# State-space layers: every state product summed by accumulating transposes, z projected in its own batch

## The reference, cut to what matters

```python
xz = xn @ in_proj; x_in, z = split(xz)            # 512 channels each
u  = silu(causal_conv4(x_in) + conv_b)
dt_r, B, C = split(u @ x_proj)                    # 64, 16, 16
dt = softplus(dt_r @ dt_proj + dt_b); A = -exp(A_log)
h  = h * exp(dt * A) + (dt * u) * B               # scan over tokens, 16 states a channel
y  = sum_n h[n] * C[n] + u * D
out = x + gate * ((y * silu(z)) @ out_proj)
```

## Time and profile before

| | us |
|---|---|
| median of 3 runs | 3429.45 |
| span of the profiled execution | 3412.4 |
| PE / DVE / ACT / POOL busy | 2677.2 / 2564.3 / 2151.3 / 1715.5 |

### The profile page before, as it was taken

The page is one execution under the profiler, slowest core; times in us unless marked ns, Lnnn a source line. Parts: engine busy times, 40 slices in busy tenths (PEclk is TensorE's granted clock), DMA queues, the critical chain, the costliest instruction groups (busy, mean ns, idle before and its releaser), DMA issues. The chain is left out here.

```text
span 3412.4 us, 37646 instructions
## 1 busy us (share of the span) xinstructions
PE 2677.2 (78%) x11156; PEld 1441.3 (42%) x11156; DVE 2564.3 (75%) x3375; ACT 2151.3 (63%) x3536; POOL 1715.5 (50%) x1221
## 2 busy tenths in 40 slices
PE   5787588888888888838888888848877788787875
PEld 4555244444444444422333333224444444444443
DVE  2444288888888898947777777538988888888895
ACT  0333478878878778613555555547876776767772
POOL 0000077867768778930000000027887877877785
PEclk9999699999999999967998989969999899989998
DMA  2000101011111111135444444010111111111111
GB/s 89 25 25 31 66 32 51 32 52 49 42 51 40 44 39 52 39 69 82 76 76 76 75 76 70 20 66 32 48 41 58 53 47 53 40 58 51 41 61 45
DMA packets 104194, 176.59 MB, mean 52 GB/s; under 512 B 10741, under 2 KB 91421, under 8 KB 95166
## 3 DMA queue, kind: packets, MB, share of 16 engines
q1 hardware_dynamic: 99775, 161.69, 17.7%
q0 software_dynamic: 4224, 12.59, 1.2%
HBM read 139.70 MB, written 34.14 MB: 51 GB/s over the span
## 5 line engine op out<-in xcount | busy, mean ns | idle before, releaser
L1037 POOL TENSOR_TENSOR l_h<-l_h,l_c_all 128x512 f32<-128x512 f32 x1024 | 1481.3, 1457 | 459.0 <-DVE l_h L966 430.8
L966 DVE TENSOR_TENSOR_SCAN l_h<-l_dA,l_ps_dbu 128x512 f32<-128x512 f32 x1024 | 1218.3, 1207 | 254.1 <-PE l_ps_dbu L1196 157.2
L838 ACT ACTIVATE l_dub<-l_duT,l_b_tok 128x512 f32<-128x512 f32 x1024 | 726.0, 713 | 336.7 <-PE l_ps_dbu L1196 330.6
L1196 PE MATMUL l_ps_dbu<-ident,l_dub 128*128 128x128 f32 x4096 | 644.7, 291 | 257.6 <-DVE l_h L966 175.6
L1196 PEld LDWEIGHTS l_ps_dbu<-ident,l_dub 128*128 128x128 f32 x4096 | 500.7, 148 | 683.6 <-DVE l_h L966 331.9
L852 ACT ACTIVATE l_dA<-l_dt,l_a_neg 128x512 f32<-128x512 f32 x1024 | 726.4, 713 | 0.2
L1628 ACT ACTIVATE l_probs<-l_ring 128x512 f32<-128x512 f32 x512 | 284.2, 598 | 301.4 <-PE l_ring L1752 298.7
L1183 PE MATMUL l_ps_y<-l_h,ident 128*128 128x512 f32 x768 | 430.2, 644 | 51.9 <-DVE l_h L931 51.4
L1461 DVE TENSOR_REDUCE l_q_max<-l_ring 128x1 f32<-128x512 f32 x512 | 327.5, 681 | 144.1 <-PE l_ring L1745 139.4
L996 POOL DMA_INDIRECT l_x_in<-x_dram,l_idx_x x32 | 37.3, 1166 | 735.9 <-DMA l_idx<-in_idx 729.6
L931 DVE TENSOR_TENSOR l_h<-l_h 128x512 f32<-128x512 f32 x384 | 350.5, 916 | 11.8 <-POOL l_h L1037 11.3
(11 more groups left out here) (237 smaller groups left out, 3000.9 us busy)
## 6 DMA issues: line engine op xcount, KB each, us to landing
...
```

Of the source, the lines that this page charges most:

```text
L838: return act.activation(dub[:, n % 2, t, :], duT[:, p, t, :], ACT.Copy, scale=b_tok[:, p, t, n:n + 1])
L966: dve.tensor_tensor_scan(h[:, h_slot(s), :], dA[:, s % DA_RING, :], ps_dbu[:, dbu_slot(s), :], 0.0, ALU.mult, ALU.add).then_inc(scan_ok, 1)
L1037: pool.tensor_tensor(h[:, h_slot(s), :], h[:, h_slot(s), :], c_all[:, (n // C_GROUP) % 2, n % C_GROUP, :], ALU.mult).then_inc(hc_ok, 1)
L1196: last = pe.transpose(ps_dbu[:, dbu_slot(s), t * P:(t + 1) * P], dub[:, n % 2, t, j * P:(j + 1) * P], ident[:])
```

## The change

`DIRECT`, the pairs and `add_states` go. `sum_states` now handles every unit by `add_turned`: four 128x128 transposes with the product as the stationary operand, which PE accumulates into `ps_y`. `ps_y` is thereby token-major. `SUM_LAG` is 9, and `h` has a ring of 16 slots (`H_RING`) where it had 12. The D term is `u *= D` on POOL in units 52 to 55 (`skip_term`), added by one more `add_turned` per block. `u` has one buffer instead of two. `z` is projected token-major inside its own batch (PE units 0, 2, 4, 6; ACT copies in 1, 3, 5, 7; SiLU in unit 32). `y_gate` comes behind the scans of units 5 to 8, and its token-major result is turned back by PE (`y_turn`, units 14, 18, 22, 26) and copied by ACT (`turned`, units 16, 20, 24, 28). The steps of the next batch keep their unit numbers.

```diff
 UNITS = N * JB
-DA_RING, DBU_RING = 8, 3
-PAIRED = UNITS // 2
-ADD_LAG, SUM_LAG = 3, 7
+DA_RING, DBU_RING, H_RING = 8, 3, 16
+SUM_LAG = 9
...
 def h_slot(s):
 
-    n, j = s // JB, s % JB
-    return 2 * JB + j if n % 2 else n // 2 % 2 * JB + j
...
+    return s % H_RING
...
-        u = sb("u", [P, 2, JB, T])
-        z = sb("z", [P, 2, JB, T])
+        u = sb("u", [P, JB, T])
+        z = sb("z", [P, 2, TB, DI])
...
-        diag_d = sb("diag_d", [P, JB, P])
...
-        h = sb("h", [P, 3 * JB, T])
+        h = sb("h", [P, H_RING, T])
...
-                def z_part(b, p, j):
-                    act.wait_ge(in_mm, b * 2 * JB + 2 * j + 2)
-                    if j == 0:
+                def z_part(b, p, t):
+                    act.wait_ge(z_mm, b * TB + t + 1)
+                    if t == 0:
                         if not early(b):
                             act.wait_ge(y_ok, b * JB - JB)
-                    act.activation(z[:, p, j, :], bank(b, "z", j), ACT.Copy).then_inc(z_ok, 1)
-
-                def silus(b, p):
+                    act.activation(z[:, p, t, :], misc[:], ACT.Copy).then_inc(z_ok, 1)
+
+                def silu_u(b):
                     act.wait_ge(conv_ok, b * JB + JB)
-                    act.activation(u[:, p, :, :], work[:], ACT.Silu).then_inc(u_ok, 1)
-                    act.wait_ge(z_ok, b * JB + JB)
-                    act.activation(z[:, p, :, :], z[:, p, :, :], ACT.Silu).then_inc(u_ok, 1)
-                    act.preload_act_table_set(EXP_LN)
+                    if not first(b):
+                        act.wait_ge(sum_ok, b * UNITS - UNITS + JB + H_RING)
+                    act.activation(u[:], work[:], ACT.Silu).then_inc(u_ok, 1)
+
+                def silu_z(b, p):
+                    act.wait_ge(z_ok, b * TB + TB)
+                    act.activation(z[:, p, :, :], z[:, p, :, :], ACT.Silu).then_inc(zs_ok, 1)
+
+                def turned(b, j):
+                    act.wait_ge(y_tr, b * JB + j + 1)
+                    act.activation(y[:, j, :], misc[:], ACT.Copy).then_inc(yd_ok, 1)
...
-                    if s in (16, 20, 24, 28): z_part(b, p, (s - 16) // 4)
-                    if s == 32: silus(b, p)
...
+                        if s in (1, 3, 5, 7): z_part(b, p, s // 2)
+                        if has_post and s in (16, 20, 24, 28): turned(b - 1, (s - 16) // 4)
+                        if s == 32:
+                            if has_prep:
+                                silu_u(b + 1)
+                            silu_z(b, p)
+                            act.preload_act_table_set(EXP_LN)
...
+                for j in range(JB):
+                    turned(B - 1, j)
...
                 def y_gate(b, p, j):
-                    dve.wait_ge(sum_ok, b * PAIRED + PAIRED - JB + j + 1 + CREDIT)
+                    dve.wait_ge(sum_ok, b * UNITS + UNITS - JB + j + 1 + H_RING)
                     if j == 0:
                         dve.wait_ge(out_mm, b * OUT_PARTS + 1)
-                        dve.wait_ge(u_ok, b * 2 + 2)
-                    dve.tensor_tensor(y[:, j, :], ps_y[:, j, :], z[:, p, j, :], ALU.mult).then_inc(y_ok, 1)
-
-                def add_states(b, s):
-                    if s // JB % 2 and s % JB != DIRECT:
-                        q, s0 = pair_of(s)
-                        dve.wait_ge(hc_ok, b * UNITS + s + 1 + CREDIT)
-                        dve.tensor_tensor(h[:, h_slot(s0), :], h[:, h_slot(s0), :], h[:, h_slot(s), :], ALU.add).then_inc(add_ok, 1)
+                        dve.wait_ge(zs_ok, b + 1)
+                    dve.tensor_tensor(y[:, j, :].rearrange("p (t c) -> p t c", c=P), ps_y[:, j, :].rearrange("p (t c) -> p t c", c=P),
+                                      z[:, p, :, j * P:(j + 1) * P], ALU.mult).then_inc(y_ok, 1)
...
                 def post_step(s, b, p):
-                    if s < ADD_LAG: add_states(b, UNITS - ADD_LAG + s)
-                    if s in (4, 5, 6, 7): y_gate(b, p, s - 4)
                     if s in (49, 52): out_gate(b, p, (s - 49) // 3)
...
                         dve.wait_ge(da_ok, b * UNITS + s + 1)
                         dve.wait_ge(dbu_ok, b * UNITS + s + 1 + CREDIT)
-                        if s // JB % 2 and s % JB == DIRECT:
-                            dve.wait_ge(sum_ok, b * PAIRED + pair_of(s)[0] - JB + 1 + CREDIT)
-                        elif s // JB % 2:
-                            dve.wait_ge(add_ok, b * ADDED + adds_before(pair_of(s)[0]) - (JB - 1) + 1 + CREDIT)
-                        else:
-                            dve.wait_ge(sum_ok, b * PAIRED + pair_of(s + JB)[0] - 2 * JB + 1 + CREDIT)
+                        dve.wait_ge(sum_ok, b * UNITS + s + 1)
                         dve.tensor_tensor_scan(h[:, h_slot(s), :], dA[:, s % DA_RING, :], ps_dbu[:, dbu_slot(s), :],
                                                0.0, ALU.mult, ALU.add).then_inc(scan_ok, 1)
-                        if s >= ADD_LAG:
-                            add_states(b, s - ADD_LAG)
+                        if has_post and s in (5, 6, 7, 8): y_gate(b - 1, 1 - p, s - 5)
...
+                for j in range(JB):
+                    y_gate(B - 1, (B - 1) % 2, j)
...
+                def skip_term(b, j):
+                    pool.wait_ge(xd_mm, b + 1)
+                    pool.wait_ge(du_ok, b * JB + j + 1)
+                    pool.sem_inc(passed_p, 1)
+                    pool.tensor_scalar(u[:, j, :], u[:, j, :], vec(vecs, L + "_D")[:, j:j + 1], None, ALU.mult).then_inc(skip_ok, 1)
...
+                        if has_prep and s in (52, 53, 54, 55): skip_term(b + 1, s - 52)
...
-                def in_proj(b, e):
...
-                    elif e < JB:
-                        pe.wait_ge(z_ok, b * JB + e)
+                    elif after_post:
+                        pe.wait_ge(yd_ok, (b - 2) * JB + e)
                     else:
-                        pe.wait_ge(xc_ok, b * JB + e - JB + 1)
+                        pe.wait_ge(xc_ok, b * JB + e)
                     for k in range(DH):
-                        last = pe.matmul(bank(b, "x", e) if e < JB else bank(b, "z", e - JB), w_in[:, k, e * P:(e + 1) * P], modT[:, k, :], start=(k == 0), stop=(k == DH - 1))
+                        last = pe.matmul(bank(b, "x", e), w_in[:, k, e * P:(e + 1) * P], modT[:, k, :], start=(k == 0), stop=(k == DH - 1))
...
-                def z_proj(b, e):
-                    in_proj(b, JB + e)
-
-                def x_proj(b, p, half):
+                def z_proj(b, t):
+                    if t == 0:
+                        pe.wait_ge(duT_ok, b * TB + TB)
+                    else:
+                        pe.wait_ge(z_ok, b * TB + t)
+                    for k in range(DH):
+                        last = pe.matmul(misc[:], modT[:, k, t * P:(t + 1) * P], w_in[:, k, DI:2 * DI], start=(k == 0), stop=(k == DH - 1))
+                    last.then_inc(z_mm, 1)
+
+                def y_turn(b, j, x_too):
+                    pe.wait_ge(y_ok, b * JB + j + 1)
+                    if x_too:
+                        pe.wait_ge(xc_ok, (b + 2) * JB + j + 1)
+                    elif j:
+                        pe.wait_ge(yd_ok, b * JB + j)
+                    elif isinstance(b, int) and b == B - 1:
+                        pe.wait_ge(og_ok, b * OUT_PARTS)
+                    else:
+                        pe.wait_ge(z_ok, b * TB + 2 * TB)
+                    for t in range(TB):
+                        last = pe.transpose(misc[:, t * P:(t + 1) * P], y[:, j, t * P:(t + 1) * P], ident[:])
+                    last.then_inc(y_tr, 1)
...
+                        pe.wait_ge(u_ok, b + 1)
+                        if after_post:
+                            pe.wait_ge(yd_ok, b * JB - JB)
+                        else:
+                            pe.wait_ge(xc_ok, b * JB + JB)
...
+                    elif isinstance(b, int) and b >= B - 2:
+                        pe.wait_ge(yd_ok, b * JB + JB)
                     else:
-                        pe.wait_ge(y_ok, b * JB + JB)
+                        pe.wait_ge(yd_ok, b * JB + JB)
                         pe.wait_ge(dti_ok, b * JB + 3 * JB)
...
-                    if s in (14, 18, 22, 26): z_proj(b, (s - 14) // 4)
...
-                def skip_term(b, p, j):
-                    if first(b):
-                        if j == 0:
-                            pe.wait_ge(diag_ok, 1)
-                    else:
-                        pe.wait_ge(y_ok, b * JB - JB + j + 1)
-                    pe.matmul(ps_y[:, j, :], diag_d[:, j, :], u[:, p, j, :], start=True, stop=False, skip_group_check=True)
-
-                def sum_states(b, p, s):
+                def add_turned(j, src, start, stop):
+
+                    for t in range(TB):
+                        last = pe.matmul(ps_y[:, j, t * P:(t + 1) * P], src[:, t * P:(t + 1) * P], ident[:], is_transpose=True,
+                                         start=(start and t == 0), stop=stop, skip_group_check=True)
+                    return last
+
```

(26 more changed lines are left out.)

54 lines of the change are left out of this document (22 added, 32 removed).

## The result

The changed kernel takes 3225.7 us (median of 4 runs, 3217.9 to 3237.6) against 3427.0 for the kernel before on the same chip: ratio 0.9421, 95% interval 0.9394 to 0.9447. It is 201 us faster; 301 were forecast (3126). 3226 lies inside the range of 3050 to 3270, but 100 us from the forecast. Its profiled execution has a span of 3220.6 us.

A forecast was written before the change was run, and what follows sets the result against it. No engine bounds the whole run; each stretch has its own bound. Batches of 113.0 (L1, from 133.7) and 117 (L3, from 140.3), gains trimmed by 0.7, give 298, plus 5 elsewhere: span 3109, plus 17 is 3126 us, range 3050 to 3270.

The forecast's parts named there:

- The pair additions, and the taps: DVE loses 22 us of additions a batch; with taps at 0.64, units 15 to 31 take 28.5 us (37.1 before).
- Rival 2: In units 15 to 31 POOL delays every tap by 1.04, 16.6 us more a batch; 3361 us, chance 0.08.
- The price of an accumulating transpose: PE's state sums: 0.44 us for four accumulating transposes, other bound 0.86; 29.9 us a batch (37.8 before).
- The clock: PE keeps its full clock while running mostly transposes, against the skill's rule; no time was added for it.
- Rival 3: Transposes do not hold PE's full clock, so the kernel gets slower; about 3770 us, chance 0.06.
- z in its own batch, units 0 to 12 at 22: z's projections and copies move into units 0 to 7; units 0 to 12 take 22 us (21.5 before), no gain.
- Rival 4: Sum right per engine, but waits between engines keep 5 us more a batch; 3196 us, chance 0.27.
- D on POOL: Units 52 to 55: four instructions at 1.0, 4 us; POOL falls 4.6 us behind, catches up later, off the path.
- rival 1: On PE four accumulating transposes cost 0.86; gains of 11.5 and 14 a batch; 3245 us, chance 0.12.
- the gathers ... and taps out of step: A batch of L3 takes 4 us more than one of L1: 117 us, with POOL another 9 us behind.
- Outside the batches: Last batches lose additions but gain a tail of about 5 us, batch 0's preparation loses z: together 5 us gained.
- the 17 us between span and median: Added to the forecast span of 3109 us to give the forecast time of 3126 us.

The follow-up runs named there:

- e7: e1 with the state sums as plain fp32 multiplications by the identity in place of accumulating transposes: 3345.4 us.
- e1: The changed kernel with the layer norm's one shift operation on DVE written as four single-input TENSOR_SCALARs of 128x1: 3169.2 us.
- e5: e1 with L3's row-number update at unit 32 and its four gathers of x at unit 33, in place of units 16 to 24: 3136.9 us.
- e4: The changed kernel with half of z's multiplications left out, so z is only a partial sum: 3217.3 us.
- e11: e5 with z's projections at units 1, 3, 5, 7 in place of 0, 2, 4, 6, and its copies one unit later: 3137.0 us.
- e3: The changed kernel without POOL's multiplication of u by D; u is added as it is: 3155.8 us.
- e6: e1 with D back on PE as four plain multiplications of 128 columns, in place of POOL's multiplications and accumulating transposes: 3159.5 us.
- e8: The changed kernel with the edits of e1, e5 and e6 together: 3136.1 us.
- e9: e5 with the four multiplications of u by D moved from POOL to DVE, at units 56 to 59: 3150.5 us.

## Why the prediction was right or wrong

**The pair additions, and the taps: right.** Units 15 to 31 were to be 28.5 and are 28.2 in L1; a tap is 0.64 behind a scan. Rival 2's price of 1.04 on every tap did not come. ACT is the busiest engine of the L1 batch above with 107.1 us in all, as forecast (PE 103.5, DVE 97.6, POOL 101.3).

**The price of an accumulating transpose: right.** 0.44 for four, the nearest row's value, and not the 0.86 of the other bound; e7 shows what the other end would have cost. In the changed kernel L1177 accumulates and L1202 does not:

```profile
1157.77 0.60 PE L1177 MATMUL l_ps_y<-ident,l_h 128*128 128x128 f32 x4
1158.20 0.60 PE L1202 MATMUL l_ps_dbu<-ident,l_dub 128*128 128x128 f32 x4
1158.64 0.60 PE L1177 MATMUL l_ps_y<-ident,l_h 128*128 128x128 f32 x4
```

**The clock: right.** Stretches in which PE ran mostly transposes stand at 1.00, 2.4 GHz (4.80 busy of 4.80 in units 12 to 15). The changed kernel also has a second clean case beside that of the earlier trace rows. PE had idled 3.99 us, up to 1147.78, for want of `dub` behind the standing shift, and then the clock fell; PE ran nothing but transposes from 1147.78 to 1156.05, up to 1152.0 mostly at 1.2 GHz, and behind them the clock was back at 2.4 GHz:

```profile
1148.60:1152.00 3.40, 3.40 (x18) 3.40 (x17) 3.40 (x5) 3.40 (x7) 2.55 (x2) 0.50 0.00 0
1152.00:1156.30 4.30, 4.30 (x39) 4.24 (x39) 2.79 (x3) 4.19 (x7) 3.00 (x4) 1.00 0.02 4
```

Rival 3, the rule of the Trainium skill in "TensorE: Matmul & The Clock Gate", Part 4, would have made the kernel slower; the trace disagrees with it.

**z in its own batch, units 0 to 12 at 22: right as a sum, wrong as a stretch.** Where the shift does not stand, the stretch takes 21.1 to 21.8 (e1, e5). With it 25.9 and 30.1. Rival 4 had 5 us more a batch and 3196, 30 us from the result and the nearest of all. It named no wait. What cost the time is DVE standing beside POOL; rival 2 has that, but at the taps and for one product each, and neither has it at the shift. e4 and e11 find no other wait that matters in this stretch.

**The step that failed: D on POOL, "POOL falls 4.6 us behind ... and catches up in units 0 to 12. Off the path."** Its price was too low first: 1.57 each, above the upper bound of 1.24, so 6.3 a batch and not 4. No run has it at 4. But the size alone is not the point: e1 leaves POOL its load, and units 0 to 12 are back at 21.5 and 21.8; e3 takes D away whole, and the shift still stands 4.6 to 6.4 us in four batches of L3. What failed is "off the path". I asked only whether a semaphore waits for POOL. The backlog means that POOL's products follow each other without a pause, and the shift, shut out by one product, was then shut out by all of them, 5.4 to 11.2 us in ten batches. Before the change DVE's additions waited for POOL at a distance of three units, and at unit 4 the shift took 0.14; that the one is the reason for the other is argued and not shown.

**That 3226 lies in the range is luck as to the mechanism.** The range was wide for dearer transposes (rival 1) and for waits without a name (rival 4). The stall at the shift, which cost the time, was in none of its terms.

**The rows for it stood in the prediction.** The tap of 1.68 in the earlier trace rows stood beside one product, and rival 2 priced it as 1.04, the rest of one product, for each tap. The two additions of 7.24 in the earlier trace rows I read as "because POOL is behind". The idle time before them is 1.62; the 7.24 themselves are busy time. The two of them, by duration (least, median, most in ns), and the timeline there in the kernel before, of POOL and of PE's weight loads:

```profile
L931 DVE TENSOR_TENSOR l_h<-l_h x2: 679/3656/6633, 3262.1 to 3268.7; 128x512 f32<-128x512 f32 x2
...
3259.57 3.73 POOL L1037 TENSOR_TENSOR l_h<-l_h,l_c_all 128x512 f32<-128x512 f32 x3
3263.25 1.26 POOL L1019 TENSOR_TENSOR l_res<-l_res,l_og 128x512 f32<-128x512 f32 x1
3264.48 1.25 POOL L1037 TENSOR_TENSOR l_h<-l_h,l_c_all 128x512 f32<-128x512 f32 x1
3265.70 1.26 POOL L1019 TENSOR_TENSOR l_res<-l_res,l_og 128x512 f32<-128x512 f32 x1
3266.93 1.25 POOL L1037 TENSOR_TENSOR l_h<-l_h,l_c_all 128x512 f32<-128x512 f32 x1
3268.79 0.50 PEld L1183 LDWEIGHTS l_ps_y<-l_h,ident 128*128 128x128 f32 x2 [5.90 <-DVE l_h L931]
```

The first addition, begun at 3262.10, stands through the product in progress and four more operations of POOL back to back, up to 3268.18. It ends 6.63 us after its start, 0.55 behind them, and PE goes on. Ten times the 0.68 of its neighbour was the sign.

**L3, "the gathers ... and taps out of step", 4 us: right for the taps, too little in all.** Units 15 to 31 are 3.7 longer than in L1, all in two first taps behind a gather (e5 moves them away). The gathers of y and the residuals at the end of the batch were not priced for what they do to the next one: the shift stands 10.7 to 11.2 us in four of the seven batches there, where it stands 5.4 to 7.5 in L1. A batch of L3 is 6.9 longer than one of L1 and not 4.

**Outside the batches.** The forecast had 5 us of gain there; the profiles have 1510.5 us outside them before and 1518.7 after, 8 us of loss. And the 17 us between span and median were taken for time around the instructions. In each run whose execution time stands beside its span the difference is 1.6 to 3.5 us (3222.3 and 3220.6 for the changed kernel), so most of the 17 was only that the profiled execution before was shorter than the median one. It moves the forecast by little: the gains of 303 off the median of 3427 give 3124.

**Left open.** Units 12 to 15 take 6.2 where the shift does not stand. PE waits there for ACT's copy `modT`, 1.1 us in each of the 14 batches of e1, and never for POOL:

```profile
1136.13 1.98 PE L1082 MATMUL l_misc<-l_modT,l_w_in 128*128 128x512 f32 x4 [1.08 <-ACT l_modT L761]
```

e3, with 6.3 us less for POOL, keeps the 6.2 in all of L1, so it is not POOL's load; e6 and e8, with D on PE, have 4.8 and no such wait, but lose more in units 0 to 12. This is a small case of rival 4, and no run takes it away by itself.

When a run of POOL shuts DVE out is not settled either. In three batches the shift took only 0.46 or 0.47, although POOL's next product followed without a pause; its scan had ended only 0.3 us before it, so POOL was not behind. In L1 of e9 POOL was behind, and DVE got in all the same.

No kernel had the additions or the place of z changed alone, so how the 201 us divide between them is argued from the stretches and not shown.
